# A graph stage with its threshold search stepped by GpSimd and its symmetric sum made in PSUM

## The reference

```
sim = jnp.einsum('bhnd,bhmd->bnm', Q, K) / (jnp.sqrt(jnp.float32(d)) * H)
k = max(1, int(n * TOP_K_RATIO))                      # 153 of 512
threshold = jax.lax.top_k(sim, k)[0][:, :, -1:]
sparse_mask = (sim >= threshold).astype(sim.dtype)
A_learned = jax.nn.sigmoid(sim) * sparse_mask
A_learned = (A_learned + jnp.swapaxes(A_learned, -1, -2)) * 0.5
gamma = jax.nn.sigmoid(gamma_raw)
graph = (1.0 - gamma) * x + gamma * A_learned         # adj_raw is x
x = layernorm(x + graph)
```

## Time and profile before

| | us |
|---|---|
| median of 3 runs | 2621.11 |
| lowest and highest of them | 2618.74, 2622.66 |
| the profiled execution, its own time | 2620.35 |
| its span in the trace | 2618.3 |
| PE, DVE, ACT, POOL busy in the span | 2004.7, 1760.9, 1258.8, 718.3 |

### The profile page before, as it was taken

How to read it: one execution, slowest core, us unless ns; L and a number is a source line. 1 busy time by engine, 2 the same in 40 slices (tenths; PEclk the granted TensorE clock), 3 DMA queues, 4 the chain that set the end, 5 groups by cost and what they waited for, 6 DMA issues and landing times. The chain is left out here.

```text
span 2618.3 us, 32959 instructions
## 1 busy us (share of the span) xinstructions
PE 2004.7 (77%) x12124; PEld 1350.8 (52%) x12156; DVE 1760.9 (67%) x2783; ACT 1258.8 (48%) x2244; POOL 718.3 (27%) x662
## 2 busy tenths in 40 slices
PE   5999999377778785888894699999910279879990
PEld 4778777222222221455552578777610157657770
DVE  3446565376768685799997445556568865379986
ACT  2323232177556564477777232323348541169881
POOL 1111222203595930211111120232200004055535
PEclk8899999688889888999996699999965589889995
DMA  5332321555352420400000432323110030099976
GB/s 153 83 72 53 70 60 39 159 149 152 85 157 73 147 51 10 175 1 1 1 1 1 121 71 52 73 50 74 25 64 0 0 116 1 1 387 422 415 285 192
DMA packets 84584, 264.55 MB, mean 101 GB/s; under 512 B 17504, under 2 KB 19040, under 8 KB 73424
## 3 DMA queue, kind: packets, MB, share of 16 engines
q0 software_dynamic: 29632, 151.50, 17.3%
q1 hardware_dynamic: 53776, 110.75, 14.9%
q10 hardware_dynamic: 1024, 0.26, 0.0%
HBM read 169.87 MB, written 41.72 MB: 81 GB/s over the span
## 5 line engine op out<-in xcount | busy, mean ns | idle before, releaser
L919 DVE TENSOR_REDUCE x_negm<-x_M 128x2 f32<-128x1024 f32 x256 | 309.3, 1223 | 111.3 <-PE x_M L979 110.8
L868 ACT ACTIVATE x_PT<-x_T 128x512 f32<-128x512 f32 x512 | 280.0, 598 | 197.3 <-PE x_T L999 192.0
L326 ACT ACTIVATE L_attn_PT<-L_attn_T 128x512 f32<-128x512 f32 x320 | 175.7, 595 | 359.5 <-PE L_attn_T L557 359.4
L407 DVE TENSOR_REDUCE L_attn_negm<-L_attn_M 128x2 f32<-128x1024 f32 (+1 forms) x192 | 192.2, 1040 | 58.6 <-PE L_attn_M L538 58.5
L233 POOL DMA_DIRECT2D L_attn_QKS<-L_attn_HL x64 | 34.9, 545 | 596.9 <-ACT L_attn_HL L311 563.1
L999 PE MATMUL x_T<-x_QS,x_KS 49*128 49x512 f32 x512 | 140.0, 544 | 64.7 <-ACT x_PT L868 44.9
L555 PE MATMUL L_attn_T<-L_attn_QKS 97*128 97x256 f32 (+3 forms) x512 | 166.8, 387 | 8.3 <-DMA L_attn_QKS<-L_attn_mT 6.2
L999 PEld LDWEIGHTS x_T<-x_QS,x_KS 49*128 49x128 f32 x512 | 51.8, 199 | 213.3 <-ACT x_PT L868 131.6
L536 PE MATMUL L_attn_M<-L_attn_QKS 96*128 96x384 f32 (+2 forms) x384 | 139.6, 434 | 28.8 <-DVE L_attn_XTL L381 11.5
L1008 PE MATMUL x_O<-x_PT,x_V 128*32 128x512 f32 x1024 | 153.4, 673 | 8.6 <-issue 8.4
L979 PE MATMUL x_M<-x_KS,x_QS 48*128 48x512 f32 x512 | 118.3, 459 | 42.6 <-DMA x_QS<-x_xl 22.8
(11 more groups left out here) (389 smaller groups left out, 5528.3 us busy)
## 6 DMA issues: line engine op xcount, KB each, us to landing
L_attn_QKS<-L_attn_HL SPq DMA_DIRECT2D x192, 128.0 KB, 4.7
L_attn_QKS<-L_attn_HL POOLq DMA_DIRECT2D x192, 128.0 KB, 4.1
moe_y_rows<-slots_YS SPq DMA_DIRECT2D x47, 256.0 KB
x_WRAW<-in_w_gateT POOLq DMA_DIRECT2D x8, 1024.0 KB, 7.2
x_QS<-x_xh SPq DMA_DIRECT2D x128, 64.0 KB, 2.4
x_WRAW<-in_w_upT POOLq DMA_DIRECT2D x8, 1024.0 KB, 5.2
x_WRAW<-in_w_downT POOLq DMA_DIRECT2D x8, 1024.0 KB, 6.2
ffn_w<-x_WTER POOLq DMA_DIRECT2D x12, 512.0 KB, 3.5
```

What stands on the lines that cost most here:

```text
L326: ac.activation(PT[:, s, bank], T[:, bank], ACT.Exp, scale=SCALE).then_inc(t_free, 1)
L407: last = ve.tensor_reduce(negm[:, g % 2, h0:h0 + nh, i], src, AX.X, ALU.max, negate=True)
L868: ac.activation(PT[:, s // 4, head(s), :], T[(STEPS_S * g + s) % 3][:], ACT.Exp, scale=SCALE).then_inc(t_free, 1)
L919: ve.tensor_reduce(negm[:, g % 2, u // 4:4:2, u % 4], m[:].rearrange("p (r k) -> p r k", r=2), AX.X, ALU.max, negate=True).then_inc(m_free, 1)
```

## The change

Three things change. First, `WS` has four entries: Wv and Wo in the first place of `PT`, Wq in the memory of `V`, Wk in the second place of `PT`. Wk is fetched without a wait, Wo when the low part of Wv is made. The first "v" unit on DVE waits for the low part of Wq.

Second, the search: POOL keeps `mid`, `low`, `width` and `take`. The 16 columns are in two sides, `side(col, g)`, each with four tiles of DVE and four of ACT. DVE and ACT count side 0, then side 1, while POOL steps the other. Behind each halving POOL scales one tile of x by g2 in place. gamma is loaded ahead of SIM, and its sigmoid stands ahead of the counts. The loops are written out.

Third, the batches: `L` has two places and DVE masks batch b + 1 before the z of batch b. PE writes into a bank first `ident` times `L` (512 columns) and adds the four transposed blocks as ordinary products with `ident`. DVE makes z straight from that bank and from x. `SUM` and `XS` are gone, and four PSUM tiles are used in turn.

```diff
         WS = [PT[:, 2 * r:2 * r + 2, :].rearrange("p a n -> p (a n)").rearrange("p (k n) -> p k n", k=KC)
               for r in range(2)]
+        WS = [WS[0], V[:], WS[1], WS[0]]
...
-        w_in = [sem("w_in0"), sem("w_in1")]
+        w_in = [sem(f"w_in{w}") for w in range(4)]
...
             sp.dma_start(WS[1], wts[ORDER[1]]).then_inc(w_in[1], 16)
-            for w in range(2, 4):
-                sp.wait_ge(w_lo, w - 1)
-                sp.dma_start(WS[w % 2], wts[ORDER[w]]).then_inc(w_in[w % 2], 16)
+            sp.dma_start(WS[2], wts[ORDER[2]]).then_inc(w_in[2], 16)
+            sp.wait_ge(w_lo, 1)
+            sp.dma_start(WS[3], wts[ORDER[3]]).then_inc(w_in[3], 16)
...
-                    act.wait_ge(w_in[w % 2], 16 * (w // 2 + 1))
-                    ac.activation(WH[:, ORDER[w]], WS[w % 2], ACT.Copy).then_inc(w_hi, 1)
+                    act.wait_ge(w_in[w], 16)
+                    ac.activation(WH[:, ORDER[w]], WS[w], ACT.Copy).then_inc(w_hi, 1)
...
                     ve.tensor_tensor(WL[:, ORDER[w]].rearrange("p k n -> p (k n)"),
-                                     WS[w % 2].rearrange("p k n -> p (k n)"),
+                                     WS[w].rearrange("p k n -> p (k n)"),
...
                     if kind == "v" and arg == (0, 0, 0):
+                        dve.wait_ge(w_lo, 2)
                         dve.wait_ge(b_in, 32)
...
-        L = sb("L", [P, NT, S], F32)
-        SUM = sb("SUM", [P, NT, S], F32)
-        XS = sb("XS", [P, NT, S], F32)
+        L = sb("L", [P, 2, NT, S], F32)
...
+        HALF = DVE_TILES // 2
+        side = lambda col, g: col[:].rearrange("p (e t) -> p e t", e=2)[:, :, HALF * g:HALF * (g + 1)]
...
         @block.sync
         def _(sp):
+            sp.dma_start(graw[:], A["gamma"]).then_inc(q["loaded"], 16)
             for b in (0, 2, 1, 3):
                 sp.dma_start(SIM[:, NT * b:NT * (b + 1), :].rearrange("p i s -> p (i s)"), GR["sim"][b]).then_inc(sim_in[b], 16)
-            sp.dma_start(graw[:], A["gamma"]).then_inc(q["loaded"], 16)
+
+        @block.gpsimd
+        def _(pool):
+            PER = 6
+            for g in range(2):
+                gp.tensor_tensor(side(mid, g), side(low, g), side(width, g), ALU.add).then_inc(q["mid_made"], 1)
+            for n in range(HALVINGS):
+                for g in range(2):
+                    step = Steps(pool, q["halving"], 2 * n + g, PER)
+                    pool.wait_ge(q["counted_v"], 2 * n + g + 1)
+                    step(gp.tensor_scalar(side(take, g)[:, 0], side(count, g)[:, 0], TOPK - 0.5, None, ALU.is_ge))
+                    pool.wait_ge(q["counted_a"], 2 * n + g + 1)
+                    step(gp.tensor_scalar(side(take, g)[:, 1], side(count, g)[:, 1], S + 1.5 - 2 * TOPK, None, ALU.is_le))
+                    step(gp.tensor_tensor(side(take, g), side(take, g), side(width, g), ALU.mult))
+                    step(gp.tensor_tensor(side(low, g), side(low, g), side(take, g), ALU.add))
+                    step(gp.tensor_scalar(side(width, g), side(width, g), 0.5, None, ALU.mult))
+                    step(gp.tensor_tensor(side(mid, g), side(low, g), side(width, g), ALU.add))
+                    pool.sem_inc(q["mid_made"], 1)
+                if n == 0:
+                    pool.wait_ge(q["gam2"], 2)
+                gp.tensor_scalar(XF[:, n, :], XF[:, n, :], g2[:, 0:1], 1.0, ALU.mult, ALU.mult).then_inc(q["scaled"], 1)
...
-            with t.Fori(0, NB) as b:
+            for b in range(NB):
                 t.wait_ge(q["masked"], b * NT + NT)
                 for v in range(2):
-                    t.wait_ge(q["summed"], b * 2 + v)
+                    if b >= 2:
+                        t.wait_ge(q["z_done"], (b - 2) * NT + 2 * v + 2)
                     for j in range(2):
                         i = 2 * v + j
+                        both = PP[(2 * b + v) % 4][:, BANK * j:BANK * (j + 1)]
+                        pe.matmul(both, C["ident"][:], L[:, b % 2, i, :], start=True, stop=False)
                         for m in range(NT):
-                            last = pe.transpose(PP[2 * v][:, BANK * j + P * m:BANK * j + P * (m + 1)],
-                                                L[:, m, P * i:P * (i + 1)], C["ident"][:])
+                            last = pe.matmul(both[:, P * m:P * (m + 1)], L[:, b % 2, m, P * i:P * (i + 1)], C["ident"][:],
+                                             start=False, stop=(m == NT - 1))
                     last.then_inc(q["turned"], 1)
...
         def _(act):
+            act.wait_ge(q["loaded"], 16)
+            ac.activation(gamma[:], graw[:], ACT.Sigmoid).then_inc(q["gam"], 1)
             for b in range(DVE_TILES // NT, NB):
                 act.wait_ge(sim_in[b], 16)
-            with act.Fori(0, HALVINGS) as n:
-                act.wait_ge(q["mid_done"], n + 1)
-                for t in range(DVE_TILES, NTILE):
-
-                    inst = ac.activation(seen_a[:, t - DVE_TILES, :], SIM[:, t, :], ACT.Sign, scale=-1.0,
-                                         bias=mid[:, t:t + 1], accum_out=count[:, t:t + 1])
-                inst.then_inc(q["counted_a"], 1)
-            act.wait_ge(q["loaded"], 16)
-            ac.activation(gamma[:], graw[:], ACT.Sigmoid).then_inc(q["gam"], 1)
+            for n in range(HALVINGS):
+                for h in range(2):
+                    act.wait_ge(q["mid_made"], 2 * n + h + 1)
+                    for t in range(DVE_TILES + HALF * h, DVE_TILES + HALF * (h + 1)):
+                        inst = ac.activation(seen_a[:, t - DVE_TILES, :], SIM[:, t, :], ACT.Sign, scale=-1.0,
+                                             bias=mid[:, t:t + 1], accum_out=count[:, t:t + 1])
+                    inst.then_inc(q["counted_a"], 1)
             for b in range(DVE_TILES // NT):
                 act.wait_ge(sim_in[b], 16)
...
@@ -1593,10 +1619,6 @@
                     act.wait_ge(q["masked"], b * NT)
                 for i in range(NT):
                     ac.activation(SIGM[:, i, :], SIM[:, b * NT + i, :], ACT.Sigmoid).then_inc(q["sigm"], 1)
-                if b:
-                    act.wait_ge(q["z_done"], b * NT)
-                for i in range(NT):
-                    ac.activation(XS[:, i, :], XF[:, b * NT + i, :], ACT.Identity, scale=g2[:, 0:1]).then_inc(q["xs"], 1)
             act.wait_ge(q["shifted"], 1)
...
-            with dve.Fori(0, HALVINGS) as n:
-                k = Steps(dve, q["halved"], n, 4)
-                ve.tensor_tensor(mid[:], low[:], width[:], ALU.add).then_inc(q["mid_done"], 1)
-                dve.wait_ge(q["mid_done"], n + 1)
-                for t in range(DVE_TILES):
...
-                inst.then_inc(q["counted_v"], 1)
-                dve.wait_ge(q["counted_v"], n + 1)
-                k(ve.scalar_tensor_tensor(out=take[:, 0:DVE_TILES], in0=count[:, 0:DVE_TILES], scalar=TOPK - 0.5,
...
-                                          op0=ALU.is_le, op1=ALU.mult))
-                k(ve.tensor_tensor(low[:], low[:], take[:], ALU.add))
-                k(ve.tensor_scalar(width[:], width[:], 0.5, None, ALU.mult))
-                k.done()
-            dve.wait_ge(q["gam"], 1)
-            pre = Steps(dve, q["gam2"], 0, 2)
-            pre(ve.tensor_scalar(g2[:], gamma[:], -1.0, 2.0, ALU.mult, ALU.add))
-            pre(ve.tensor_scalar(gh[:], gamma[:], 0.5, None, ALU.mult))
+            for n in range(HALVINGS):
+                for h in range(2):
+                    dve.wait_ge(q["mid_made"], 2 * n + h + 1)
+                    for t in range(HALF * h, HALF * (h + 1)):
+                        inst = ve.tensor_scalar(seen_v[:, t, :], SIM[:, t, :], mid[:, t:t + 1], 0.0, ALU.is_ge, ALU.add,
+                                                accum_out=count[:, t:t + 1])
+                    inst.then_inc(q["counted_v"], 1)
+                if n == 0:
+                    dve.wait_ge(q["gam"], 1)
+                    pre = Steps(dve, q["gam2"], 0, 2)
+                    pre(ve.tensor_scalar(g2[:], gamma[:], -1.0, 2.0, ALU.mult, ALU.add))
+                    pre(ve.tensor_scalar(gh[:], gamma[:], 0.5, None, ALU.mult))
+            dve.wait_ge(q["mid_made"], 2 * HALVINGS + 2)
...
+            def mask(b):
+                if b >= 2:
+                    dve.wait_ge(q["turned"], 2 * (b - 1))
+                for i in range(NT):
+                    t = b * NT + i
+                    dve.wait_ge(q["sigm"], t + 1)
+                    ve.scalar_tensor_tensor(out=L[:, b % 2, i, :], in0=SIM[:, t, :], scalar=low[:, t:t + 1],
+                                            in1=SIGM[:, i, :], op0=ALU.is_ge, op1=ALU.mult).then_inc(q["masked"], 1)
+
+            mask(0)
             for b in range(NB):
-                if b:
-                    dve.wait_ge(q["turned"], b * 2)
+                if b + 1 < NB:
+                    mask(b + 1)
+                else:
+                    moments(0, 0, EARLY)
                 for i in range(NT):
-                    dve.wait_ge(q["sigm"], b * NT + i + 1)
```

(27 more changed lines are left out.)

11 lines of the change are left out of this document (2 added, 9 removed).

## The result

The changed kernel took 2591.86 us (median of 4 runs, 2584.59 to 2607.48), the kernel before 2621.89 us beside it (4 runs, 2618.74 to 2627.80). The ratio is 0.9887, with a 95% interval of 0.9854 to 0.9920: 30.0 us less by the medians. The profiled execution took 2594.45 us, with a span of 2592.7 us.

A forecast was written before the change was run, and what follows sets the result against it. The kernel was taken as a row of stages with barriers, each change worth what it takes off its stage. Search -20.6, batches -13.3 and attention 0 gave -33.9 us: 2587.2 from a median of 2621.11, range 2579 to 2607.

The forecast's parts named there:

- The sum: Whole kernel: search -20.6, batches -13.3 and attention 0 make -33.9 us, giving a median of 2587.2 us.
- the likeliest case: Whole kernel: the main forecast, 68 in 100, likeliest 2587 us, own range 2581 to 2594.
- Attention: 0: Both attention stages: earlier Wk gains 0, bounds -0.3 to +0.3 us, since DVE's V units stand ahead of `WL`.
- The search: 20.6: Graph stage search: POOL's chain fits under ACT's other half, ACT runs without pause, first mask 20.6 us earlier.
- The batches: 13.3: Graph stage after the search: PE sums in PSUM and masks run ahead, 55.1 us becomes 41.8, 13.3 less.
- the rise of PE's clock: Batches: PE goes from 1.2 to 2.4 GHz 3.5 us into unbroken work; range used for the clock step 3.1 to 3.7.
- The list of times: Batches: schedule from first mask to last statistics, 41.8 us, with DVE idle twice in batch 0 and hardly later.
- The clock stays low: Rival, batches: PE stays at 1.2 GHz, batches cost 5.5 us more than before, total 2606; 8 in 100.
- 128-column products dearer than a quarter: Rival, batches: PE's 128-column products take 0.32 us, PE becomes the bound, 3 us later, 2590; 9 in 100 with dear scaling.
- Dear scaling: Rival, search: POOL's scaling takes 2.07 us, load 6.1, 6 us of gain lost, 2593; shares the 9 in 100.
- POOL's steps slowed by DVE's counting: Rival, search: slowed small steps, total 2590 to 2637; 15 in 100, 5 of them slower than before.
- the loss beyond 7.84 us: Search, within the slowed-POOL rival: the change loses against the kernel before once a halving's period passes 7.84 us.

The follow-up runs named there:

- the second: The changed kernel measured once more beside the kernel before: 2573.05 us against 2606.47, ratio 0.9870; graph stage 156.0 us.
- Warm PE: The changed kernel with 24 spare PE products ahead of the first masks: one execution, graph stage 153.2 us, 2.9 less than the changed kernel.
- masks in turn: The changed kernel with each batch's masks directly ahead of its own z: ratio to before 0.9944; graph stage 173.8 us, 17.7 more than the changed kernel.
- no accumulator: The changed kernel with DVE comparing without writing counts, in a plain form lacking the second operation: one execution, graph stage 156.0 us.
- dear scaling: The changed kernel with POOL's scaling of X in a two-pointer form: ratio to before 0.9886; graph stage 160.3 us, 4.2 more than the changed kernel.
- graph stage alone: The changed kernel with the attention weight places of before: 2574.27 us, ratio to before 0.9876; graph stage 156.1 us.
- start early: The changed kernel with SIM fetched in order 2, 0, 3, 1 and first-halving halves each awaiting their own batch: one execution, graph stage 152.4 us.
- batches alone: The kernel before with the new batches behind its old search, and all 16 scalings on POOL at once: ratio 0.9952; graph stage 176.9 us.
- all three: The changed kernel with reordered SIM and per-batch waits, a shortened last halving, and spare PE products: 2580.49 us against 2617.63, ratio 0.9860; stage 148.2 us.
- end early: The changed kernel without width and mid in the last halving, first masks awaiting half 0, scaling between chains: one execution, graph stage 153.6 us.

## Why the prediction was right

**The sum.** -33.9 was predicted; -30.0 was measured in the first comparison and -33.4 in the second. The graph stage gave -32.5: the search gave 0.6 more than its term and the batches 2.0 less, so part of the error cancelled by luck. Against the -32.5 stand the 6.6 us that the profiled execution took longer ahead of it, for which the experiments found no cause in the change beyond, perhaps, the 1.2 us of the V units in attention. The median of 2591.86 lies in the likeliest case's own range of 2581 to 2594.

**Attention: 0.** The mechanism is right: PE's 3.07 us wait stands, behind DVE's order. That the effect lies within 0.3 us can't be shown: in the first attention stage of the changed kernel's profile what follows the V units lies 1.2 us later, by a clock that rose later, with a spread of 1.4 us over the kernels with the new places; the run with the places alone bounds it by -1 and +5 us.

**The search: 20.6.** Measured 113.68 - 91.98 = 21.7 less between ACT's first count and the first mask, and 0.5 lost at the start, as foreseen (first count 12.5 us after the stage's first issue before, 13.0 after): 21.2. The period was 5.64 us (90.2/16) where 5.67 was taken; POOL's steps took 0.20 to 0.24 and its chain 2032.0 - 2030.4 = 1.6 from ACT's last count, where 1.7 was taken; the scaling 0.695. The 0.6 us more are the shorter period (0.5) and the 0.2 taken here for the collision of last scaling and first mask. The collision came and cost 0.45, but it lengthens the masks and so lies in the next stretch.

**The batches: 13.3.** Measured 11.3. The term that was mis-sized is the rise of PE's clock: 3.5 us into unbroken work was taken, from a single rise in the stage behind. The row itself gives 3.7 ((1 - 0.54) x 4 / 0.5 from 2110) and not the 3.4 of the lower bound. Here it came 5.8 us after PE's start, and in the repetitions with this code 5.9 to 6.1. By the working's own formula the first unit then ends (5.8 - 3.5)/2 = 1.15 later, and the 0.45 of the longer masks come on top: 1.6 of the 2.0 missing. Of the last 0.4, the moments of 12 tiles took 5.6 us up to the next z (2064.66 to 2070.24) where 5.3 was taken; the rest lies ahead of the first z, where a bank took 3.57 us at the low level and not 3.43. The list of times otherwise held: DVE idle twice in batch 0 (3.27 and 0.65 us) and nowhere later, as written. *Warm PE* shows that the start was the cost, and *masks in turn* that the whole gain of this part hangs on the order of the masks, which hides PE's first units and keeps its clock up. One rise in one trace was too little for the bound of 3.1 to 3.7 us that the prediction put on it.

**The rivals.** *The clock stays low*: it did not; *masks in turn* is the nearest thing to it, 17.7 us dearer. *128-column products dearer than a quarter*: a bank is 1.75 us against 1.72, so no. *Dear scaling*: priced at 6 us, and the search lost 5.2, since POOL's load came to 5.99 and not 6.1 us. *POOL's steps slowed by DVE's counting*: not with the accumulator form (231 ns), and *no accumulator* shows that the other form does it (374). That a slowed POOL sets the period above its slack was shown by *dear scaling*; the loss beyond 7.84 us was not reached by any run.

## What to carry to other kernels

When two engines search in lock-step and a chain of small steps stands between rounds, split the columns in two and give the steps to a third engine: the chain is hidden as long as it is shorter than half a round, here 1.6 of 2.8 us, and its slack (about 1 us in a round) is what may be given to other work. Work moved to PE from a slower engine is worth what PE's clock at that place makes it worth: look at what PE did in the microseconds ahead, order its input so that it never stops, and give it something to do before the first piece. To judge parts of a change of 1%, read the length of the stage in the profile: it repeated to 0.1 us, where the whole time needed several runs for a few us. Then look for what in the stage is chance: here PE's clock rose 3.8 to 6.2 us after a start, and that alone moved the stage by up to 1 us.

## What had not been expected of the hardware

The clock's rise had no one delay from PE's start in these runs: 5.8 us after it in the changed kernel and 5.9 to 6.1 in its repetition, *graph stage alone*, *no accumulator* and *start early*, but 4.9 in *batches alone*, 4.4 in *dear scaling*, about 4.6 with the spare products (start 2024.9, and 0.62 over 2028 to 2030) and 5.1 with them in *all three*, and some 3.8 in *end early* and in the second batch of *masks in turn*. In the V units of attention, by the distance of the products, it was 2.9 to 6.3 us. The first z moved with it by 1 us. What sets the delay stays open.

POOL's work beside a DVE mask, which reads two tensors from SBUF, was held up in both cases seen, but the mask in one only: the 0.69 us scaling took 1.19 and the 0.73 us mask 1.18 (1.18 in each of eight profiles), whereas a small step of 0.20 took 0.73 while the masks beside it lost nothing (2.74 for four).
